# Distance stage of a three-block kernel: normalised rows and third bf16 parts on GpSimd, V product copied one slot later

## What is computed

```
x = layernorm(x)                       # per row of 128
q, k, v = x @ Wq, x @ Wk, x @ Wv       # 16 heads of 8
dist = max(|q|^2 - 2 q.k + |k|^2, 0)   # per head, 512 x 512
scores = exp(-gamma * scale * dist), kept where key > query, else 0
x0 + (scores @ v) @ Wo
```

## Time and profile before

| | |
|---|---|
| median of 3 runs | 1851.25 us (1850.41 to 1852.17) |
| the profiled execution | span 1853.5 us from its first to its last instruction; no other time of it is listed |
| busy over the span | PE 1676.8 us (90%), DVE 1449.6 (78%), ACT 1437.3 (78%), POOL 753.0 (41%) |
| the first block | about 0 to 455 us |

### The profile page before, as it was taken

The page is one execution under the profiler, slowest core; times in us unless marked ns, Lnnn a source line. Parts: engine busy times, 40 slices in busy tenths (PEclk is TensorE's granted clock), DMA queues, the critical chain, the costliest instruction groups (busy, mean ns, idle before and its releaser), DMA issues. The chain is left out here.

```text
span 1853.5 us, 67967 instructions
## 1 busy us (share of the span) xinstructions
PE 1676.8 (90%) x27513; PEld 1287.6 (69%) x27513; DVE 1449.6 (78%) x3461; ACT 1437.3 (78%) x4100; POOL 753.0 (41%) x842
## 2 busy tenths in 40 slices
PE   3888898886899999999997996879999999999797
PEld 1444444443688888888886774658888888888686
DVE  8999999998677678877887766747777777789674
ACT  4989999996788888888774666658888888877464
POOL 2010000000255444455446866425454545455694
PEclk7999999998999999999999997989999999999999
DMA  6565556551001010101012000000101010001211
GB/s 194 140 155 146 149 124 148 132 149 28 13 15 25 14 26 14 26 14 26 14 26 48 2 2 1 1 12 15 25 14 26 15 25 18 22 14 25 48 47 47
DMA packets 80040, 91.95 MB, mean 50 GB/s; under 512 B 11696, under 2 KB 67984, under 8 KB 79728
## 3 DMA queue, kind: packets, MB, share of 16 engines
q1 hardware_dynamic: 78432, 87.15, 19.0%
q10 hardware_dynamic: 1296, 0.44, 0.1%
HBM read 39.68 MB, written 31.10 MB: 38 GB/s over the span
## 5 line engine op out<-in xcount | busy, mean ns | idle before, releaser
L1519 POOL TENSOR_TENSOR f1l_pn<-f1l_p,f1l_rs 128x512 f32<-128x512 f32 (+1 forms) x256 | 207.9, 834 | 259.3 <-DVE f1l_rs L1206 258.2
L1519 POOL TENSOR_TENSOR f2l_pn<-f2l_p,f2l_rs 128x512 f32<-128x512 f32 (+1 forms) x256 | 207.9, 834 | 248.8 <-DVE f2l_rs L1206 248.7
L1078 ACT ACTIVATE f2l_p<-f2l_sm,f2l_nb 128x192 f32<-128x192 f32 x512 | 214.7, 444 | 43.9 <-DVE f2l_nb L1199 43.9
L1078 ACT ACTIVATE f1l_p<-f1l_sm,f1l_nb 128x192 f32<-128x192 f32 x512 | 214.8, 444 | 42.0 <-DVE f1l_nb L1199 42.0
L417 PE MATMUL r_acc<-r_pr,r_vp 128*32 128x128 f32 (+2 forms) x3584 | 197.9, 338 | 6.9 <-DVE r_pr L630 6.0
L527 ACT ACTIVATE r_pr<-r_far 128x1536 f32<-128x1536 f32 x128 | 195.4, 1526 | 3.3 <-PE r_far L401 3.0
L622 DVE SCALAR_TENSOR_TENSOR r_pr<-r_pr,k_lo,r_cap 128x512 f32<-128x512 f32 x256 | 180.7, 746 | 11.0 <-ACT r_pr L527 10.9
L630 DVE TENSOR_SCALAR r_pr<-r_pr,k_hi,k_lo 128x768 f32<-128x768 f32 x256 | 164.5, 684 | 0.0
L527 ACT ACTIVATE r_pr<-r_near 128x1024 f32<-128x1024 f32 x128 | 139.6, 1091 | 1.1 <-PE r_near L388 1.1
L1524 POOL MEMSET k_rtz<- 128x132 f32 x1 | 0.2, 208 | 337.3 <-POOLq L688 337.3
L417 PEld LDWEIGHTS r_acc<-r_pr,r_vp 128*32 128x32 f32 x3584 | 89.1, 112 | 49.7 <-issue 31.2
(11 more groups left out here) (505 smaller groups left out, 5158.7 us busy)
## 6 DMA issues: line engine op xcount, KB each, us to landing
rbf_rows<-r_part SPq DMA_DIRECT2D x112, 128.0 KB, 2.3
r_qs<-rbf_rows SPq DMA_DIRECT2D x60, 192.0 KB
r_ks<-rbf_rows SPq DMA_DIRECT2D x60, 192.0 KB
f1l_vs<-f1l_vv SPq DMA_DIRECT2D x64, 128.0 KB, 2.4
f2l_vs<-f2l_vv SPq DMA_DIRECT2D x64, 128.0 KB, 2.4
rbf_rows<-r_part SPq DMA_DIRECT2D x16, 384.0 KB, 3.1
rbf_rows<-r_part SPq DMA_DIRECT2D x16, 256.0 KB, 3.2
out<-k_x SPq DMA_DIRECT2D x8, 512.0 KB, 3.2
```

The source lines that it names most:

```text
L1078: ins = nc.scalar.activation(p[:, u % 2, k, :], sm[:, u % 2, k // 2, k % 2 * PW:(k % 2 + 1) * PW], ACT.Exp, bias=nb[:, u % 2, k:k + 1], ac ...
L1519: ins = nc.gpsimd.tensor_tensor(pn[:, u % 2, at:at + HU * w].rearrange("p (k c) -> p k c", k=HU), p[:, u % 2, :, cols], r.broadcast_to([P, ...
```

## The change

ACT loses `norm`, DVE loses `third_part` in the loop, and POOL gets both: for each batch from 2 on it makes `z` (four multiplications and additions, 128x128 with two scalars per partition), then, with the weight split in between for three of the batches, the three third parts (two subtractions of 128x512, one of 128x256, an f32 and a bf16 operand from SBUF, bf16 out). The third parts of batches 0 and 1 that are made ahead of the loop stay on DVE. The wait for `s_nb` goes from ACT to POOL. The copy of the V product moves from behind the far exponentials of w = 3 to between the near and the far ones of w = 4.

```diff
--- before.py
+++ after.py
@@ -217,7 +217,6 @@
         PAIRS = RH // 2
         AHEAD = {0: (1, 3), 3: (1, 4), 5: (2, 0), 6: (2, 1), 7: (2, 2)}
         OUT_AT = 4
-        NORM_AT = 4
         FRESH_AT = 3
         SPLIT_AT, THIRD = 1, H * DH
         RUN = B - 3
@@ -492,14 +491,6 @@
                 act.wait_ge(*left_by(b, k))
                 nc.scalar.activation(p[:, 1, :], left, ACT.Copy).then_inc(s_p2, 1)
 
-            def norm(b):
-                wait(act, s_mp, USES * (b - 1) + 1)
-                for j in range(NT):
-                    t = b * NT + j
-                    ins = nc.scalar.activation(z[:, j, :], K["x"][:, t, :], ACT.Identity, scale=rstd[:, t:t + 1],
-                                               bias=nbias[:, t:t + 1])
-                ins.then_inc(s_z, 1)
-
             def leave_values(b):
                 act.wait_ge(s_pv, 4 * (b + 1))
                 wait(act, s_wo, b)
@@ -536,21 +527,20 @@
                 leave(1, k)
             roots(REST, ROOTS)
             nc.scalar.preload_act_table_set("natural_log_exp_and_others")
-            act.wait_ge(s_nb, 1)
             for b in range(B):
                 for w in range(PAIRS):
                     n = PAIRS * b + w
                     wait(act, s_pv, (n - RING) // 2 + 1)
                     exps(n, slice(0, ON), near[:], s_dg, s_exd)
+                    if w and ahead(b, w - 1) and ahead(b, w - 1)[1] == USES - 1:
+                        leave(*ahead(b, w - 1))
                     exps(n, slice(ON, RCOLS), far[:, :, 0:RCOLS - ON], s_of, s_exo)
                     if w == 2 and b:
                         leave_values(b - 1)
                     if split(b, w):
                         second_part(*split(b, w))
-                    if ahead(b, w):
+                    if ahead(b, w) and ahead(b, w)[1] < USES - 1:
                         leave(*ahead(b, w))
-                    if w == NORM_AT and b < B - 2:
-                        norm(b + 2)
             leave_values(B - 1)
             nc.scalar.preload_act_table_set("sqrt_and_others")
 
@@ -660,8 +650,6 @@
                     n = PAIRS * b + w
                     masked(n)
                     bounded(n)
-                    if split(b, w):
-                        third_part(*split(b, w))
                     if ahead(b, w):
                         remainder(*ahead(b, w))
                     if w == OUT_AT and b:
@@ -679,12 +667,35 @@
             nc.gpsimd.tensor_tensor(cap[:], K["later_key"][:].unsqueeze(1).broadcast_to([P, RH, P]),
                                     K["hi"][:].unsqueeze(2).broadcast_to([P, RH, P]), ALU.mult).then_inc(s_cap, 1)
 
-            for q in range(3):
+            def norm(b):
+                pool.wait_ge(s_mp, USES * (b - 1) + 1)
+                for j in range(NT):
+                    t = b * NT + j
+                    ins = nc.gpsimd.tensor_scalar(z[:, j, :], K["x"][:, t, :], rstd[:, t:t + 1], nbias[:, t:t + 1],
+                                                  ALU.mult, ALU.add)
+                ins.then_inc(s_z, 1)
+
+            def split_weights(q):
                 w = slice(THIRD * q, THIRD * (q + 1))
                 pool.wait_ge(s_wl, 16 * (q + 1))
                 nc.gpsimd.tensor_copy(K["wqkv_h"][:, w], whole[:]).then_inc(s_wh, 1)
                 pool.wait_ge(s_wh, 2 * q + 1)
                 nc.gpsimd.tensor_tensor(K["wqkv_l"][:, w], whole[:], K["wqkv_h"][:, w], ALU.subtract).then_inc(s_wh, 1)
+
+            def third_part(b, k):
+                p, left = parts(b, k)
+                pool.wait_ge(s_p2, 3 * b + k)
+                nc.gpsimd.tensor_tensor(p[:, 2, :], left, p[:, 1, :], ALU.subtract).then_inc(s_p3, 1)
+
+            pool.wait_ge(s_nb, 1)
+            for b in range(2, B):
+                norm(b)
+                if b == 2:
+                    third_part(1, 3)
+                if 0 <= b - 3 < 3:
+                    split_weights(b - 3)
+                for k in range(1, 4):
+                    third_part(b, k)
         work.close()
         sem.end()
 
```

## The result

The changed kernel takes 1856.26 us (median of 16 runs, 1849.35 to 1863.05) against 1851.16 us before (16 runs, 1848.15 to 1855.8): ratio 1.0025, 95% interval 1.0015 to 1.0035. It is slower by a quarter of a per cent, as forecast; 1858 us was predicted, in a range of 1846 to 1871.

A forecast was written before the change was run, and what follows sets the result against it. DVE, full together with ACT, was taken to stay the bound: 25.16 - 1.54 + 2.3 = 25.9 us a batch, 0.5 more than now. Over 14 batches that is 7 us, giving a median of 1858 us, range 1846 to 1871.

The forecast's parts named there:

- Points 1 and 2: Work removed per batch: ACT loses 1.53 us, falling to 23.34; DVE loses third parts of 1.54 us, falling to 23.62.
- Point 3: POOL's third parts hold up DVE: 0.96 us per large one, 0.48 for the small, 2.40 a batch, lower end 1.80.
- Point 4: POOL's four normalisations cost DVE 0.35 us a batch, with ends of nothing and 1.40.
- Point 5: Masks and bounds, 85% of DVE's work, take the loss: (2.40 + 0.35) x 0.85 = 2.3; DVE's batch 25.9 us.
- Point 6: Moved V copy: ACT waits 0.4 us longer for the diagonal of w = 4, covered by slack under DVE's 25.9.
- Points 7 and 8: POOL's queue, 5.8 to 10 us of 25.9, and SP's transfers, `s_p3` at most 0.9 later, cost nothing.
- The three weight splits stay and cost what they did: POOL's three splits of a weight beside DVE's load keep their cost, adding nothing to the forecast sum.
- Rival A: Faster: POOL gives way, DVE loses nothing; next bound SP's loop at 24.56, just over ACT's 24.3; 1839 us; chance 0.13.
- Rival B: Slower: PE half-clock stretches in each of 14 batches instead of 6 add 13 us, 1871 us; chance 0.16.
- less than the whole: Beside POOL's weight split, DVE lost 0.35 of a 1.01 us cast and 0.96 of a 1.60 us subtraction.

The follow-up runs named there:

- with DVE freed: The changed kernel with a POOL fill (zeros, nothing read) in place of each third part: 1860.99 us in a single run.
- the version with both edits of the last section: Against the kernel with only the normalised rows moved to POOL: V product at w = 2 and the residual's sum on PE; 1851.79 us (12 runs).

## Why the prediction was right, point by point

The direction, the mechanism and the sum held: 25.9 us a batch predicted, 25.79 measured; 7 us in all, 5.1 in the medians.

- **Points 1 and 2** (work removed): DVE's third parts are gone from its rows, as forecast. ACT lost less than the 1.53 us of point 1: over a whole batch it is busy 23.95 us, 0.92 less than the 24.87 of before. Where the other 0.6 us went is open; ACT had the time to spare.
- **Point 3** took 0.96 us for a large third part, of the weight's subtraction; it is 0.85, and 0.43 for the small one: 2.14 us a batch, within the ends 1.80 and 2.40 that stood there before the factor of 0.85. Large third parts last 1.16 to 1.37 us in the undisturbed batch and at most 1.56, not 1.6: about 1.10 us and what is left of the DVE instruction under which they begin.
- **Point 4** took 0.35 us for the rows; they cost DVE 0.05. It reasoned that the hold follows the amount read. The trace of before had the better hint, POOL's 128x128 instruction stretched to 1.50 us, which is what happened here (5.77 us for four).
- **Point 5** scaled both by 0.85, for DVE's share of masks and bounds. That discount was wrong in kind: all 43 third parts started under a mask or a bound, 41 of them under a mask, as ACT's second part ended there. The two errors, a price too high and a discount that does not apply, nearly cancelled: 2.3 predicted, 2.14 + 0.05 measured. That the sum came so close is in part luck.
- **Point 6** had the wait of 0.4 us right, 0.91 for the old 0.52; ACT waits 0.91 + 0.32 + 0.32 = 1.55 us in a batch, of which the two waits of 0.32 were not foreseen. "Without that cover up to 0.4 a batch" was too simple. Alone, the copy costs 0.9%, and in its profile it does so mostly through the clock.
- **Points 7 and 8** held: from 204 to 282 us no matmul waits for POOL or for a load.
- **"The three weight splits stay and cost what they did"** is not contradicted, and not shown outright. Two splits lie between residuals of the changed kernel, each in a batch of 27.06 us at full clock, 1.27 over the undisturbed one; before, DVE lost 0.35 + 0.96 = 1.31 us to one. The batches of before with these splits, 27.04 and 27.63 us, each hold a half-clock stretch as well, so the batches themselves can't be compared.
- **Rival A's floor** (24.3 to 24.6) was wrong: with DVE freed the batch was 25.63. It added ACT's work and one wait, and left out that PE and ACT wait for each other in turn. **Rival B** did not come in the one profile of the changed kernel, but the copy alone shows it can.
- Of the shared hold, the page SBUF — State Buffer of the Trainium skill (section "SBUF: two separate sides") has whoever starts first keep it for its whole instruction. The subtractions nearly agree: of the bounds at 196.47 only the first instruction is longer, by 0.86 us, where by the rule it would have lost the 1.11 us left of the third part that began at 196.21. The prediction's "less than the whole" set the loss against POOL's full time, in which POOL's own wait stands: the subtraction of the earlier trace rows began 0.39 us before the bounds of the earlier trace rows, so 1.21 of its 1.60 us lay beside them, and 0.96 was lost. Both times the loss is 0.25 us short of the whole; why is not shown. The rows do not agree: over 5.77 us DVE began nine instructions beside the four of them and lost 0.05. So who pays depends on the POOL instruction; whether by its operands, its columns or its operation, no run separates.

## What to carry to other kernels

Moving work from a full DVE to an idle POOL pays only if DVE loses less under POOL's instruction than the instruction cost at home: here a subtraction of 512 columns saved DVE 0.60 us and cost it 0.85, while four 128x128 scalings from ACT cost it 0.05. Read that price from any place in the trace where both already work side by side, before moving anything. And before costing what a freed engine gives, look for the loop of the other two: their waits for each other do not go away when the third has time.

## What the runs showed that was not expected

- A loop that repeats exactly can lock onto the half clock: with the copy alone, every batch from 152.9 us on has one 3.4 us stretch at 0.5, and is 27.31 us long where the undisturbed batch of before is 25.40. The changed kernel, with the same copy and a slower DVE, has two such stretches.
- POOL's instruction with two operands in SBUF holds DVE up (0.85 us of 1.16 to 1.37), its scaling of one operand with two scalars is held up by DVE (1.44 us each, 0.45 undisturbed). In the version with both edits of the last section, where DVE has pauses, the four rows take 2.40 us in a batch, 0.60 each.
